# A transformer layer with a mixture of experts: three units' rows sorted by expert and computed in 15 groups of 256

## The chip, the cores and the metric

The kernel runs on one core of a Trainium2 chip. The metric is the device time of one execution in microseconds. Its engines are TensorE (PE in the rows, its weight loads PEld), VectorE (DVE), ScalarE (ACT), GpSimd (POOL) and the queue of SyncE (SP), each with its own instruction queue that it works through in order. Engines wait for each other through semaphores.

## What is computed

16 sequences of 128 tokens (2048 rows of 192 numbers) pass an embedding, an attention layer with 8 wide heads, a second attention ("mixer") with 12 heads of 16, a dense feed-forward layer and a mixture of experts. The change touches the last one alone:

```python
xm = _ln(x, ln2_g, ln2_b)
logits = xm @ gate_w.T + gate_b                  # 4 experts
topv, topi = jax.lax.top_k(logits, TOPK)         # TOPK = 2
gates = jax.nn.softmax(topv, axis=-1)
comb = ...                                       # gates spread over the 4 experts, 0 for the two not chosen
for e in range(NEXP):                            # NEXP = 4
    he = jax.nn.gelu(xm @ exp_w1[e] + exp_b1[e], approximate=False)   # 192 -> 768
    oe = he @ exp_w2[e] + exp_b2[e]                                    # 768 -> 192
    moe_out = moe_out + comb[..., e:e + 1] * oe
return x + moe_out
```

Every row needs only two of the four experts; the reference computes all four and multiplies two of them by zero.

## The kernel before

**Tiles and units.** The 2048 rows are 16 tiles of 128 rows, 4 units of 4 tiles (`UNIT = 4`, so 512 rows). Attention comes first; `mixer_and_feed_forward` does the rest, in one block. Its work is cut in named steps, and the order of the steps on each engine is written out by hand for the first part (`ORDERS`, one list each for pe, act, dve and pool) and made by a rule for the rest (`order`, with the additional steps of `after` hung behind chunks).

**Precision.** A factor in 32 bits is split in a high part of a narrower type (`fp32r`) and the rest (`_hi`, `_lo`). Layer 1 of an expert (L1) is five matmuls of 512 rows for each chunk of 128 hidden values; there are 6 chunks (`HC = 6`). ScalarE then takes the gelu from PSUM (L1426) and makes the high part (L1430), VectorE subtracts to get the low part (L1570). Layer 2 (L2) is, for each of 4 tiles, one matmul against 384 columns (L1335, both parts of w2) and one against 192 (L1336), summed over the 6 chunks in the four banks of `ps_out`. Behind the sixth chunk VectorE adds the result, weighed by `gates`, to `total` in 8 operations (step EF, L1635 to L1639).

**Experts.** `ffns` lists 4 units x 4 experts, `chunks` has 96 entries: all units meet all experts. L2 runs two chunks behind L1 (`LAG = 2`). `hid_hi` and `hid_lo` have 3 buffers, `gelu` has 2, and all that TensorE writes besides `ps_scores`/`ps_out` goes through a ring of 4 PSUM banks (`slot_free` waits until the bank is emptied).

**Routing a unit.** EN normalises its rows (VectorE: bias, moments, 13 small steps of a root, then 4 scalings that write `xn`), EX transposes them (PE), scales and splits them (ACT L1412, L1414, DVE L1566), EG makes the logits, EB turns them back and subtracts the largest, RANK finds the two largest, EXP is the exponential (ACT, with a table load before it and one behind), GATES makes the weights. For units 1 to 3 these steps are spread over the last expert of the unit before and the first of its own. WEIGH sums the experts' output biases by the gates, on GpSimd (L1142, L1144). B adds the rows saved earlier (`h1`, loaded by SP) to the residual (L1132); the single buffer `h1` is loaded for the next unit only behind B of this one (`base_ready`).

**Weights.** SP loads the weights of the dense layer and the experts one after the other in `stage` and `stage2`; H (GpSimd, L1116 to L1120) and W (DVE, L1488) split them. `load_weights(f)` waits until the f-th earlier set is split (`weights_lo`). At the end `store` and four DMAs write `total` to `out`.

## Time and profile before

| | us |
|---|---|
| median of 3 runs | 876.88 (876.34 to 877.64) |
| the profiled execution | 875.9 |
| its span, first to last instruction | 874.1 |
| TensorE busy | 792.7 (91%) |
| VectorE busy | 534.2 (61%) |
| ScalarE busy | 475.8 (54%) |
| GpSimd busy | 275.1 (31%) |

The profile shows one execution. Busy times say which engine is short of time over the whole; a change in one stage has to be read from the time in which it lies. The stages on the clock of the trace: attention to about 423 us, mixer and dense layer from there to about 657, mixed with the first experts of unit 0 from 619, and experts alone to 871. A matmul row shows a start and a length; matmuls overlap, so the distance between starts is what one costs.

### The profile page before, as it was taken

The page shows a single profiled execution, that of the slowest core. Times are in us where ns is not written, and L with a number is a line of the kernel's source. Part 1 is how long each engine was busy: PE and PEld are TensorE (multiplying, and loading weights), DVE is VectorE, ACT ScalarE, POOL GpSimd, SP SyncE. Part 2 cuts the span into 40 slices and gives each one's busy share as a digit, 9 for nine tenths or more (in the row PEclk, how much of TensorE's full clock was granted, in tenths as well). Part 3 has the DMA queues.
Part 4 walks back from the last instruction along what each step waited for, and adds up shares of the span by engine and source line. Part 5 has one row for each costly group of instructions (what it writes and reads, how often), then busy time and mean ns, then how long its engine had stood idle before and what let it go on. Part 6 is the DMA issues. An engine that isn't in the chain of part 4 may idle for free.

```text
span 874.1 us, 16507 instructions
## 1 busy us (share of the span) xinstructions
PE 792.7 (91%) x6000; PEld 716.2 (82%) x6000; DVE 534.2 (61%) x1404; ACT 475.8 (54%) x1292; POOL 275.1 (31%) x483
## 2 busy tenths in 40 slices
PE   0398999999999999998388799999989999999998
PEld 0298999999999999997367688888888898888987
DVE  4855545546454545426587688765677766775565
ACT  2155444444544454543078488997635575666654
POOL 6363020201111110202133745555376053070060
PEclk9989999999999999999699699999999999999999
DMA  8253333241413142333402002000040000100000
GB/s 254 90 118 73 73 82 74 72 84 55 93 55 86 34 109 47 73 82 73 137 1 64 2 1 65 1 20 2 15 124 8 1 19 3 35 0 1 18 2 18
DMA packets 37505, 47.32 MB, mean 54 GB/s; under 512 B 4721, under 2 KB 32497, under 8 KB 37425
## 3 DMA queue, kind: packets, MB, share of 16 engines
q1 hardware_dynamic: 34608, 42.03, 19.1%
q0 software_dynamic: 944, 2.16, 1.0%
q10 hardware_dynamic: 1872, 2.08, 0.9%
q8 instruction: 48, 0.79, 0.4%
q14 instruction: 33, 0.26, 0.1%
HBM read 30.53 MB, written 15.73 MB: 53 GB/s over the span
## 4 chain that ended last, share of the span: by engine, by line
PE 37%; DVE 5%; POOL 4%; DMA 2%; ACT 2%; issue 1%; SPq 0%; ACTq 0%; DVEq 0%; POOLq 0%
PE mix_ring L1320 11%; PE mix_scores L1335 7%; PE mix_scores L1336 3%; PE mix_ring L1262 2%; PE mix_ring L1211 2%; PE mix_ring L1233 2%; PE mix_ring L1274 2%; PE mix_scores L1200 1%; PE mix_ring L1173 1%; POOL mix_bias_part L1142 1%; DMA mix_stage<-in_w 1%; PE mix_ring L1224 1%; ACT mix_probs L1377 1%; POOL mix_bias_sum L1144 1%; DMA mix_w_out<-in_w_mix_out 1%
## 5 line engine op out<-in xcount | busy, mean ns | idle before, releaser
L454 POOL TENSOR_SCALAR attn_probs<-attn_probs,attn_inverse 128x128 f32<-128x128 f32 x128 | 47.8, 374 | 288.3 <-DVE attn_inverse L744 280.5
L1570 DVE TENSOR_TENSOR mix_hid_lo<-mix_gelu,mix_hid_hi 128x512 fp32r<-128x512 f32 x96 | 80.5, 840 | 68.2 <-ACT mix_hid_hi L1430 67.4
L1335 PE MATMUL mix_scores<-mix_w,mix_hid_hi 128*128 128x384 f32 x384 | 115.9, 359 | 0.4 <-DVE mix_hid_lo L1570 0.3
L1426 ACT ACTIVATE mix_gelu<-mix_ring,mix_b 128x512 f32<-128x512 f32 x96 | 65.7, 684 | 86.4 <-PE mix_ring L1320 79.6
L1336 PE MATMUL mix_scores<-mix_w,mix_hid_lo 128*128 128x192 f32 x384 | 96.5, 251 | 0.0
L1102 POOL TENSOR_SCALAR mix_probs<-mix_probs,mix_inverse 128x128 f32<-128x128 f32 x192 | 73.5, 403 | 65.9 <-DVE mix_inverse L1528 65.9
L613 ACT ACTIVATE attn_probs<-ps_scores,attn_neg_max 128x128 f32<-128x128 f32 x128 | 45.2, 366 | 77.8 <-DVE attn_neg_max L740 77.8
L1335 PEld LDWEIGHTS mix_scores<-mix_w,mix_hid_hi 128*128 128x128 f32 x384 | 72.2, 188 | 5.8 <-DVE mix_hid_lo L1570 1.6
L1336 PEld LDWEIGHTS mix_scores<-mix_w,mix_hid_lo 128*128 128x128 f32 x384 | 73.1, 190 | 3.3
L1377 ACT ACTIVATE mix_probs<-mix_scores,mix_neg_max 128x128 f32<-128x128 f32 x192 | 67.6, 389 | 1.9 <-DVE mix_neg_max L1520 1.8
L1142 POOL TENSOR_SCALAR mix_bias_part<-mix_b,mix_gates 128x192 f32<-128x192 f32 x64 | 38.4, 614 | 94.7 <-DVE mix_gates L1606 93.6
L1430 ACT ACTIVATE mix_hid_hi<-mix_gelu 128x512 fp32r<-128x512 f32 x96 | 60.8, 633 | 9.8 <-PE mix_scores L1336 6.9
L627 ACT ACTIVATE attn_mixed_rows<-ps_mixed 128x512 f32<-128x512 f32 x32 | 19.3, 604 | 84.6 <-PE ps_pairs L544 84.6
L751 DVE COPY attn_mixed_rows<-ps_pairs 128x256 f32<-128x256 f32 x32 | 13.6, 424 | 66.4 <-PE ps_pairs L544 66.4
L559 PE MATMUL ps_scores<-w_proj_main,attn_mixed_rows 128*128 128x192 f32 x256 | 44.4, 326 | 2.5 <-issue 1.8
L559 PEld LDWEIGHTS ps_scores<-w_proj_main,attn_mixed_rows 128*128 128x128 f32 x256 | 41.8, 190 | 3.4 <-issue 2.0
L1377 ACT ACTIVATION_READ_ACCUMULATOR mix_probs<-mix_scores,mix_neg_max 128x1 f32 x192 | 44.2, 230 | 0.0
L1320 PE MATMUL mix_ring<-mix_xt_hi,mix_w_hi 128*128 128x512 f32 x96 | 40.7, 424 | 0.8 <-DVE hin L1556 0.8
L736 DVE TENSOR_TENSOR attn_v_flat<-ring,attn_b_v 128x512 f32<-128x512 f32 x48 | 32.8, 684 | 8.5 <-PE ring L503 8.3
L1320 PE MATMUL mix_ring<-mix_xt_lo,mix_w_hi 128*128 128x512 f32 x96 | 37.9, 394 | 0.0
L1320 PE MATMUL mix_ring<-mix_xt_lo,mix_w_stack 128*128 128x512 f32 x96 | 37.8, 394 | 0.0
L1320 PE MATMUL mix_ring<-mix_xt_hi,mix_w_stack 128*128 128x512 f32 x96 | 37.7, 392 | 0.0
(292 smaller groups left out, 2373.7 us busy)
## 6 DMA issues: line engine op xcount, KB each, us to landing
v_rows<-attn_v_flat SPq DMA_DIRECT2D x16, 768.0 KB, 3.3
attn_v_rows<-v_rows SPq DMA_DIRECT2D x128, 96.0 KB, 3.7
mix_stage<-in_w SPq DMA_DIRECT2D x5, 576.0 KB, 5.8
mix_stage<-in_w SPq DMA_DIRECT2D x10, 192.0 KB, 3.2
mix_stage<-in_w SPq DMA_DIRECT2D x5, 384.0 KB, 4.3
attn_stage_main<-in_w_qkv SPq DMA_DIRECT2D x2, 768.0 KB, 6.8
h_rows<-hin SPq DMA_DIRECT2D x8, 192.0 KB, 2.0
mix_h<-h_rows SPq DMA_DIRECT2D x4, 384.0 KB, 4.9
```

The costliest lines, as they stand in the source:

```text
L454: last = nc.gpsimd.tensor_scalar(probs[:, n, j, :], probs[:, n, j, :], inverse[:, n, j:j + 1], float(D) ** -0.5, ALU.mult, ALU.mult)
L559: last = nc.tensor.matmul(out_of(b), mixed_rows[:, c, :], w, start=c == 0, stop=c == KTILES - 1)
L613: last = nc.scalar.activation(probs[:, n, j, :], ps_scores[:, n % 2, j, :], ACT.Exp, bias=neg_max[:, n, j:j + 1], accum_out=sums[:, n, j:j ...
L1102: last = nc.gpsimd.tensor_scalar(turn, turn, inverse[:, i, s:s + 1], 1.0, ALU.mult, ALU.mult)
L1142: last = nc.gpsimd.tensor_scalar(bias_part[:, b, :], b2[:, 1 + e, :], gates[:, b, e:e + 1], 1.0, ALU.mult, ALU.mult)
L1320: last = nc.tensor.matmul(ring[:, bank("L1", i), :], w[:, cols], x[u % XSETS][:, part, :], start=n == 0, stop=n == 4)
L1335: nc.tensor.matmul(ps_out[:, b, 0:2 * D], hid_hi[:, i % 3, tile], w2[:, c, :, :], start=c == 0, stop=False)
L1336: last = nc.tensor.matmul(ps_out[:, b, 0:D], hid_lo[:, i % 3, tile], w2[:, c, 0, :], start=False, stop=c == HC - 1)
L1377: last = nc.scalar.activation(probs[:, h // 2 % 2, i, s, :], ps_scores[:, i, s * P:(s + 1) * P], ACT.Exp, bias=neg_max[:, i, s:s + 1], acc ...
L1426: nc.scalar.activation(gelu[:, i % 2, :], ring[:, bank("L1", i), :], ACT.Gelu, bias=b1[:, f * HC + c:f * HC + c + 1]).then_inc(chunk_read, 1)
L1430: nc.scalar.activation(hid_hi[:, i % 3, :], gelu[:, i % 2, :], ACT.Copy).then_inc(hi_ready, 1)
L1570: nc.vector.tensor_tensor(hid_lo[:, i % 3, :], gelu[:, i % 2, :], raw(hid_hi[:, i % 3, :]), ALU.subtract).then_inc(lo_ready, 1)
```

## The change

Unit 0 is computed as before, all rows with all four experts. Units 1 to 3 (1536 rows, 3072 pairs of row and expert) are sorted by expert in DRAM and computed in groups.

- **Routing in one place.** EX, EG, EB, RANK, EXP and GATES of units 1, 2 and 3 all hang behind the six chunks of unit 0's third expert (chunks 12 to 17). EN of unit 2 moves to the first steps. New steps: CNT (PE: 8 matmuls that count, for each row, the earlier rows that chose each expert), SLOT (8 small DVE operations that make the two slots of each row), TABLE (16 small DVE operations: expert and block of each group), SCATTER (GpSimd: 8 indirect DMAs for each unit, 128 rows of 197 numbers each: the normalised row, its 4 gates and its own number).
- **Prefill.** SP writes 28 blocks of 256 empty rows to `sorted` and one to `home`, between `load_h1(0)` and `load_weights(1)`; `pattern`, their source, lies in `xt_full`, so EX of unit 0 waits for it. `home` gets the residual rows (`set_home`).
- **Groups.** 15 groups of 256 rows. SP reads the group's block and expert from `table` into registers and loads its rows and biases (`load_group`, rows in 5 buffers). GW1 copies the expert's layer 1 weights to a fixed place: ScalarE the high part (768 columns), VectorE the two others (1536 columns). GX transposes the rows (6 matmuls), ScalarE scales and splits, VectorE subtracts. G1 is a block: two chunks of 128 hidden values x 256 rows, ten matmuls of 256 rows; G2 its layer 2, eight matmuls, with w2 addressed by a register. GF (DVE, 6 operations) makes the weighed sum with the bias, GA (GpSimd) adds it to `home` with two indirect DMAs that add; GA of a group waits until the adds of the group before have landed.
- **End.** Unit 0's fourth expert (chunks 18 to 23) is computed behind the last group; SP then copies `home` to `out` and stores unit 0. The biases of unit 0 (WEIGH) are summed in groups 2 to 5.

```diff
-        for u in range(1, UNITS):
-            i = (u - 1) * NEXP * HC + (NEXP - 1) * HC
...
+        EARLY = 3 * HC
+        put(FIRST, ("EX", (1, 0)), ("EX", (1, 1)), ("EN", (2, NORM_PARTS - 1)))
+        put(FIRST + 1, ("EG", 1), ("EN", (3, 0)), ("EN", (3, 1)))
+        put(FIRST + 2, ("EB", 1), ("RANK", 1), ("EX", (2, 0)), ("EX", (2, 1)), *(("EN", (3, part)) for part in range(2, NORM_PARTS - 1)))
+        put(FIRST + 3, ("EXP", 1), ("CNT", 1), ("SLOT", 1), ("GATES", 1), ("SCATTER", 1), ("EG", 2), ("EN", (3, NORM_PARTS - 1)), ("B", 2), ("B", 3))
+        put(FIRST + 4, ("EB", 2), ("RANK", 2), ("EX", (3, 0)), ("EX", (3, 1)))
+        put(FIRST + 5, ("EXP", 2), ("CNT", 2), ("SLOT", 2), ("GATES", 2), ("SCATTER", 2), ("EG", 3))
+        put(FIRST + 5, ("EB", 3), ("RANK", 3), ("EXP", 3), ("CNT", 3), ("SLOT", 3), ("TABLE", 0), ("GATES", 3), ("SCATTER", 3))
...
+        both = [("L1", i) for i in range(FIRST - LAG, EARLY)] + [("G1", i) for i in range(len(blocks))] + [("L1", i) for i in range(EARLY, len(chunks))]
...
+            if step == "G1":
+                g, k = blocks[i]
+                if g + 1 < SORTS and k < 2:
+                    order.append((("GW1", "GX")[k], g + 1))
...
+            def load_group(g):
+                q = sp.value_load(table[0:1, 0, g:g + 1], min_val=0, max_val=NEXP * BLOCKS_OF - 1)
...
+            for q in range(NEXP * BLOCKS_OF):
+                sp.dma_start(dram["sorted"][q * GT:(q + 1) * GT, :].rearrange("(b p) r -> p b r", p=P), pattern).then_inc(prefilled, 16)
...
+            sp.wait_ge(scattered, 16 * TWO * UNIT * SORTED)
+            sp.wait_ge(table_ready, 1)
+            for g in range(SORTS):
+                load_group(g)
+            sp.wait_ge(came_home, 16 * GROUP_TILES * SORTS)
+            sp.dma_start(dram["out"][UT:TOKENS, :], dram["home"][0:SORTED * UT, :]).then_inc(out_stored, 16)
...
+            def scatter(u):
+                pool.wait_ge(xn_ready, u + 1)
...
+                for b in range(UNIT):
+                    for k in range(TWO):
+                        nc.gpsimd.indirect_dma_start(dram["sorted"], bass.IndirectOffsetOnAxis(ap=slots_at[:, u - 1, k, b:b + 1], axis=0),
+                                                     rows_of(u)[:, b, 0:ROW], None).then_inc(scattered, 16)
...
+            def bring_home(g):
+                pool.wait_ge(group_free, GROUP_TILES * (g + 1))
...
+                    pool.wait_ge(came_home, 16 * GROUP_TILES * g)
+                for b in range(GROUP_TILES):
+                    nc.gpsimd.indirect_dma_start(dram["home"], bass.IndirectOffsetOnAxis(ap=group_rows[:, g % DEEP, b, ROW - 1:ROW].bitcast(I32), axis=0),
+                                                 group_y[:, g % 2 * GROUP_TILES + b, :], None, compute_op=ALU.add).then_inc(came_home, 16)
...
+            def group2(i):
...
+                if k == 0:
+                    expert[g] = pe.value_load(table[0:1, 1, g:g + 1], min_val=0, max_val=NEXP - 1)
...
+                        nc.tensor.matmul(to[:, 0:2 * D], hid_hi[:, mine, tile], w_all[:, bass.ds(expert[g], 1), W1 + col:W1 + col + 2 * D], start=k + c == 0, stop=False)
...
+            def put_weights(g):
...
+                nc.vector.tensor_copy(w_dense[:, g % 2, HID:W1], raw(w_all[:, bass.ds(e, 1), HID:W1].rearrange("p e n -> p (e n)"))).then_inc(weights_put, 1)
```

## Rows read from the trace of the kernel before

**Rows 1.** Windows: length, busy (count) of PE, PEld, DVE, ACT, POOL, clock, DMA share, GB/s.
```profile
478.00:486.00 8.00, 0.51 (x5) 0.30 (x3) 2.69 (x6) 1.20 (x3) 4.52 (x8) 0.74 0.35 119
486.00:495.00 9.00, 8.98 (x56) 7.70 (x57) 5.07 (x8) 4.82 (x16) 7.09 (x11) 0.50 0.00 0
...
661.00:871.00 210.00, 208.56 (x1198) 183.97 (x1197) 138.49 (x310) 125.17 (x189) 63.90 (x71) 1.00 0.03 8
```

**Rows 2.** Timeline, PE: start, length. First L1 and L2 matmul of a chunk, next chunk.
```profile
848.95 0.42 PE L1320 MATMUL mix_ring<-mix_xt_hi,mix_w_hi 128*128 128x512 f32 x1
...
850.13 0.34 PE L1335 MATMUL mix_scores<-mix_w,mix_hid_hi 128*128 128x384 f32 x1
...
851.26 0.42 PE L1320 MATMUL mix_ring<-mix_xt_hi,mix_w_hi 128*128 128x512 f32 x1
```

**Rows 3.** Timeline, PE: two neighbours of the dense layer's matmuls of 256 rows.
```profile
617.21 0.28 PE L1262 MATMUL mix_ring<-mix_dxt_hi,mix_w_hi 128*128 128x256 f32 x1
617.33 0.28 PE L1262 MATMUL mix_ring<-mix_dxt_lo,mix_w_hi 128*128 128x256 f32 x1
```

**Rows 4.** Timeline, PE: two tiles of rows turned between these two starts.
```profile
630.26 0.27 PE L1237 MATMUL mix_ring<-ident,hin 128*128 128x128 f32 x1
...
631.46 0.44 PE L1335 MATMUL mix_scores<-mix_w,mix_hid_hi 128*128 128x384 f32 x1
```

**Rows 5.** Timeline, PE: where unit 0's chunk 12 begins.
```profile
661.19 0.42 PE L1320 MATMUL mix_ring<-mix_xt_hi,mix_w_hi 128*128 128x512 f32 x1
```

**Rows 6.** Timeline, DVE: start of an EF of eight operations, and what follows it.
```profile
664.74 0.73 DVE L1636 SCALAR_TENSOR_TENSOR mix_total<-mix_scores,mix_gates,mix_total 128x192 f32<-128x192 f32 x2
...
667.40 0.69 DVE L1570 TENSOR_TENSOR mix_hid_lo<-mix_gelu,mix_hid_hi 128x512 fp32r<-128x512 f32 x1
```

**Rows 7.** Timeline, DVE: small operations, each waiting for the one before, three steps apart.
```profile
700.40 0.22 DVE L1593 TENSOR_TENSOR mix_ties<-mix_ties,mix_earlier 128x64 f32<-128x64 f32 x1
...
701.17 0.17 DVE L1596 TENSOR_SCALAR mix_chosen<-mix_rank 128x16 f32<-128x16 f32 x1
```

**Rows 8.** Timeline, POOL: indirect DMAs of the embedding, one behind the other.
```profile
4.46 0.97 POOL L414 DMA_INDIRECT hin<-in_token_emb,attn_ids  x1 [0.30 <-issue]
5.74 0.94 POOL L414 DMA_INDIRECT hin<-in_token_emb,attn_ids  x1 [0.30 <-issue]
```

**Rows 9.** DMA view: issues, KB of each, median us from issue to landing.
```profile
v_rows<-attn_v_flat SPq DMA_DIRECT2D x16, 768.0 KB, 3.3
...
mix_h<-h_rows SPq DMA_DIRECT2D x4, 384.0 KB, 4.9
...
hin<-in_token_emb,attn_ids POOLq DMA_INDIRECT x16, 4.9
...
mix_b_qk<-in_b_mix_qk ACTq DMA_DIRECT2D x1, 1.5 KB, 1.7
```

**Rows 10.** Lines view, busy and mean ns: GpSimd's B, ACT's gelu and high part.
```profile
L1132 POOL TENSOR_TENSOR hin<-hin,mix_h 128x768 f32<-128x768 f32 x4 | 7.4, 1840 | 25.8 <-DVE norm_zn L1666 25.8
...
L1401 ACT ACTIVATE mix_dgelu<-mix_ring,mix_b 128x256 f32<-128x256 f32 x48 | 19.6, 472 | 9.3 <-PE mix_ring L1262 9.1
...
L1430 ACT ACTIVATE mix_hid_hi<-mix_gelu 128x512 fp32r<-128x512 f32 x96 | 60.8, 633 | 9.8 <-PE mix_scores L1336 6.9
```

**Rows 11.** Source view: shortest, median and longest ns of a DVE copy of 256 columns.
```profile
L187 DVE COPY norm_zn<-norm_zn x4: 293/294/349, 420.3 to 512.4; 128x256 f32<-128x256 f32 x4
```

**Rows 12.** Source view: the same of the low part on DVE.
```profile
L1570 DVE TENSOR_TENSOR mix_hid_lo<-mix_gelu,mix_hid_hi x96: 674/692/2228, 622.9 to 867.9; 128x512 fp32r<-128x512 f32 x96
```

**Rows 13.** Timelines of POOL, SP, DVE: start, length; [idle before and what ended it].
```profile
433.62 1.16 POOL L1116 TENSOR_SCALAR mix_w_hi<-mix_stage 128x768 fp32r<-128x768 f32 x1 [8.20 <-DMA mix_stage<-in_w]
...
474.53 1.78 SPq L1049 DMA_DIRECT2D mix_stage<-in_w  x2
...
639.69 0.96 DVE L1488 TENSOR_TENSOR mix_w_lo<-mix_stage,mix_w_hi 128x768 fp32r<-128x768 f32 x1 [4.30 <-POOL mix_w_hi L1116]
```

**Rows 14.** Source view: L2's second matmul, with its first and last start.
```profile
L1336 PE MATMUL mix_scores<-mix_w,mix_hid_lo x384: 247/252/255, 627.0 to 869.8; 128*128 128x192 f32 x192
```

More of the change, by code:

```diff
@@ L962, in mixer_and_feed_forward, with second_of @@
         order = []
-        for i in range(FIRST, len(chunks)):
-            chunk(i)
-        for i in range(len(chunks) - LAG, len(chunks)):
-            second(i)
+        blocks = [(g, k) for g in range(SORTS) for k in range(BLOCKS)]
+        place = lambda i: i if i < EARLY else len(blocks) + i
+        both = [("L1", i) for i in range(FIRST - LAG, EARLY)] + [("G1", i) for i in range(len(blocks))] + [("L1", i) for i in range(EARLY, len(chunks))]
+        def second_of(step, i):
+            if step == "L1":
+                second(i)
+                return
+            g, k = blocks[i]
+            order.append(("G2", i))
+            if k == BLOCKS - 1:
+                order.append(("GF", g))
+                order.append(("GA", g))
+                if 2 <= g < 2 + NEXP:
+                    order.append(("WEIGH", (0, g - 2)))
+        for n, (step, i) in enumerate(both):
+            if n < LAG:
+                continue
+            if (step, i) == ("G1", 0):
+                second_of(*both[n - LAG])
+                second_of(*both[n - LAG + 1])
+                order.append(("GW1", 0))
+                order.append(("GX", 0))
+            order.append((step, i))
+            if step == "G1":
+                g, k = blocks[i]
+                if g + 1 < SORTS and k < 2:
+                    order.append((("GW1", "GX")[k], g + 1))
+            if not (step == "G1" and i < LAG):
+                second_of(*both[n - LAG])
+            if step == "L1":
+                order.extend(after.get(i, ()))
+        for step, i in both[-LAG:]:
+            second_of(step, i)
         slot_of, slots = {}, 0
         for step, i in first_steps["pe"] + order:
-            for part in range({"X": 1, "Q": 1, "V": 1, "T": HALF, "A": 1, "O": 1, "DX": 1, "D1": 1, "D2": 1, "EX": 1, "EG": 1, "EB": 1, "L1": 1}.get(step, 0)):
+            for part in range({"X": 1, "Q": 1, "V": 1, "T": HALF, "A": 1, "O": 1, "DX": 1, "D1": 1, "D2": 1, "EX": 1, "EG": 1, "EB": 1, "L1": 1, "CNT": 1, "GX": 1, "G1": 1}.get(step, 0)):
                 slot_of[step, i, part] = slots
@@ new lines, in group1 @@
+            def group1(i):
+                g, k = blocks[i]
+                n = EARLY + i
+                act.wait_ge(l1_filled, n + 1)
+                act.wait_ge(lo_ready, n - 1)
+                if k == 0:
+                    act.wait_ge(group_weights[g % 3], 32 * (g // 3 + 1))
+                for c in range(2):
+                    part = slice(c * GT, (c + 1) * GT)
+                    last = nc.scalar.activation(gelu[:, n % 2, part], ring[:, bank("G1", i), part], ACT.Gelu, bias=group_b1[:, g % 3, 2 * k + c:2 * k + c + 1])
+                last.then_inc(chunk_read, 1)
+                act.wait_ge(chunk_read, n + 1)
+                act.wait_ge(hid_used, n - 2)
+                nc.scalar.activation(hid_hi[:, n % 3, :], gelu[:, n % 2, :], ACT.Copy).then_inc(hi_ready, 1)
```

436 lines of the change are left out of this document (318 added, 118 removed), and 4 rows, old and new, of the table ORDERS.

## The prediction

> **What bounds the kernel now.** I read the windows by stage first, then TensorE's timeline inside the stage that changes. From 661 us, where chunk 12 begins [rows 5], to 871 TensorE is busy 208.6 of 210.0 us at the full clock (2.4 GHz), with VectorE at 138.5, ScalarE at 125.2 and GpSimd at 63.9 [rows 1]. So the experts cost what TensorE needs for them: every chunk taken away is worth its TensorE time, and every wait of TensorE that is put in its place costs its whole length. One chunk is 1.18 us of L1 (848.95 to 850.13) and 1.13 of L2, together 2.31 [rows 2]. All before 661 stays nearly as it is.
>
> **What is saved on TensorE.** Chunks 24 to 95 go, 72 x 2.31 = 166.3 us. In their place come 15 groups x 3 blocks = 45 blocks. A block has ten matmuls of 256 rows at a pitch of 0.12 us [rows 3], 1.20 in all, and the same eight L2 matmuls as a chunk, 1.13 to 1.16: 2.36, so 45 x 2.36 = 106.2. Turning a group's two tiles costs 1.20 us (630.26 to 631.46) [rows 4]: 15 x 1.20 = 18.0. CNT, 8 small matmuls three times, is about 3. Net saving 166.3 - 106.2 - 18.0 - 3 = 39 us, not the 38% of the expert work that fewer rows suggest, since the groups are padded (3840 rows for 3072) and turned again.
>
> **What the sorting costs between chunk 17 and the first group.** No group can start before all 24 scatters have landed, and TensorE has no other work in its queue: L2 of chunks 16 and 17 is the last. So I follow the chain through the queues, from 661.2 on.
> Prices on VectorE: a low part 0.62 back to back (0.69 alone) [rows 12]; a small operation that waits for the one before, 0.26 for 64 columns and 0.20 for 4 to 16 (701.17 - 700.40 = 0.77 for three) [rows 7]; EF 2.65 (664.74 to 667.40) [rows 6]. In order: low part 12, EX(1), EN(2) to 668.8; low part 13, EF, EG(1), the first two parts of EN(3), a weight split to 676; low part 14, EB, RANK(1), EX(2), the root of EN(3), a weight split to 683; low part 15, SLOT(1) 1.3, GATES(1) 0.8 to 686.1. TensorE alone would be at that place before 680: VectorE has become the bound, since three units' routing lies in six chunks. It goes on through EN(3), EX(3), RANK(2), SLOT(2), EB(3), RANK(3), SLOT(3), TABLE (16 operations, 3.3 us) to GATES(3) at 705.6. TensorE ends L2 of chunk 17 at about 702.5.
> GpSimd is later still. An indirect DMA occupies it every 1.28 us (4.46 to 5.74) [rows 8]; I take 1.26, the mean of three distances there. SCATTER(1) runs 686.1 to 696.2. Then B(2), 1.84 [rows 10], to 698.1. B(3) is queued right behind it, and its `h1` is loaded by SP only after B(2): issue to landing 4.9 [rows 9], so 703.1; SCATTER(2) and SCATTER(3) are queued behind that wait. B(3) to 704.9, SCATTER(2) to 715.0, SCATTER(3) to 725.1. The last one issues at 723.9 and lands 4.9 later [rows 9]: 728.8. GATES(3), at 705.6, is then long done.
> SP reads a register and loads the group's rows, between the 3.3 and the 4.9 us of larger loads [rows 9], 4.4 with the register: 733.2. TensorE turns them, 1.2; ScalarE scales and splits, 2 x 0.47 + 0.63 = 1.6 [rows 10]; VectorE 0.69: the first block starts at about **737**, after 31 us without TensorE work.
>
> **The clock.** After the stretch 478 to 486 with TensorE almost idle, the granted clock stands at 0.50 (1.2 GHz) for 9 us in which it is busy [rows 1]. An idle stretch of 31 us should do the same: 9 us at half speed, 4.5 us lost. If the clock did not fall it would be 0; I keep both ends.
>
> **The group loop.** TensorE: 106.2 + 14 x 1.2 + chunks 18 and 19 of L1, 2.3 = 125.3. New and in no row: one register read of TensorE for each group, and w2 addressed by a register. For the read the rows give nothing (the queue has it ahead) to 1.7 us (the smallest load from memory) [rows 9]; I take 0.4, two small steps of 0.2 [rows 7], since it reads a few bytes of SBUF: 6 us for 15, with 0 to 25 as ends. The addresses I take at 0, hidden behind 0.29 us for each pair of matmuls, with 16 us (0.09 for each of 180 pairs) as the upper end. A group so costs TensorE 8.3 + 0.4 = 8.7 us.
> The cover for the rest is thin. VectorE in a group: three low parts 2.1; the weight copy of 1536 columns, by the 0.29 us of 256 columns [rows 11] about 0.95, or 1.75 at the rate of a low part; the group's input and gates 1.1; GF 2.3; its register 0.4; waits 0.3: 7.1 to 8.0. ScalarE: 3 x (0.94 + 0.63) + 1.6 + 0.9 for 768 columns + 0.4 = 7.6 [rows 10]. Both are under 8.7, so I add nothing. GpSimd: GA's two DMAs 2.5 and its wait for landing, 1.26 + 4.9 = 6.2 in all, also under 8.7.
>
> The low parts show that VectorE and GpSimd stand in each other's way: median 692 ns, longest 2228 [rows 12]. The Trainium skill (SBUF — State Buffer, on the shared port pair) says that an fp32 `tensor_copy` from SBUF to SBUF locks GpSimd out, which then cannot write DMA descriptors. This speaks against the weight copies; by it each GA could be late by one copy, which its slack of 2.5 us covers, and the sum stays. The Trainium skill (DMA: Bandwidth & Descriptors, latency and other measured facts) gives a `tensor_load` a floor of about 600 ns; by that page 15 reads would be 9 us instead of 6, if they are such loads, which no row shows.
>
> **The end.** The last G2 ends at 737 + 4.5 + 125.3 + 6 = 872.8. Then L1 of chunk 20, L2 of 18 behind GF (a stall of 0.6), and the rest: 12.2 us, TensorE ends at 885.0. Before, it ended at 870.05 [rows 14] and the span at 874.1, so 4.1 more: 889.1. Beside it the way home: GF 1.7, GA's issue 1.3, landing 4.9, copy of 1.18 MB about 6 (3.3 for 0.77 MB [rows 9]), 14 us behind the last G2 against 16.3: hidden. The profiled execution's own time is 875.9 for a span of 874.1, 1.8 more: **890.9 us**, against 875.9 there, which lies 0.1% under the median.
>
> **Edits at nothing.** GpSimd's additional fills lie in the 8.2 us in which it waits for the first weights, until 433.6 [rows 13]. The prefill (5.8 MB) stands behind those loads in SP's queue, and the second weights behind it, issued at 474.5 before [rows 13]: 41 us, of which it needs 25 at the 0.77 MB in 3.3 us of [rows 9], and 41 at 140 GB/s. Without that cover GpSimd's splits and probabilities would wait and TensorE with them, microsecond for microsecond. EN(2), 5 us of VectorE, goes mostly into the 4.3 us in which it waits until 639.7 [rows 13]; at worst 3 us. WEIGH moves under the groups.
>
> **The rivals.**
> 1. *The loop is bound beside TensorE or by registers.* VectorE at 8.0 plus contention, or addresses that do not hide, at 9.6 to 10.4 us a group: 14 to 26 us more, 905 to 917. For: thin cover, in-order waits (GF stands ahead of a low part). Against: double and triple buffers. 0.18.
> 2. *The adding DMAs bound the loop.* GA waits for the group before. It decides from 8.7 us, that is from a landing of 7.4; one of the embedding's took 7.7. An add has to read `home` first. At a landing of 10 the period is 11.3: 14 x 2.6 = 36 more, 927. 0.10.
> 3. *Faster: scattering is cheap.* If GpSimd issues a scatter every 0.5 us, SCATTER(3) ends with GATES(3), at about 710, the first block starts at 722, and with registers at nothing the sum is 891 - 15 - 6 = 870. It decides below 0.7 us each. Against: all 16 rows of this kind take 0.94 or more. It also covers the case that the saving is larger than I see. 0.17.
> 4. *The low ends together* (cadence 0.95, registers 0, clock 0): 891 - 7 - 6 - 4.5 = 874, and up to 882. 0.10, half of it within 0.2%.
>
> **How the numbers follow.** My own case, 882 to 900, has 0.45. The range reaches from half of rival 3 to past rival 1: 864 to 922. A measurement of this kernel can tell about 0.2% from no change (875.1 to 878.6). Faster 0.17, within 0.2% 0.05, slower 0.78.
>
> **What would show it.** Right: TensorE idle about 30 us behind unit 0's third expert, GpSimd with 24 indirect DMAs of 1.26 us and a wait for `mix_h` between them, clock 0.5 after it, G1's first start near 737, the same step 8.7 us later in each group. Wrong: a first group before 725, or groups apart by other than 8.3 to 9.2 us; waits of VectorE or GpSimd for the adds would name rival 2, low parts that end last rival 1.

## The result and the profile after

The median is 890.52 us (889.86 to 895.3, 4 runs) against 876.61 for the kernel before beside it: a ratio of 1.0171, 95% interval 1.0133 to 1.021. (The two medians alone give 1.0159; the ratio, taken over all runs, is above it because one of the four took 895.3.) The profiled execution takes 889.86 with a span of 888.1. The sum said 890.9 and 889.1. Two of its terms were off by more than the total shows, and in opposite directions.

The page's busy times, and windows of the new kernel (length, busy and count of PE, PEld, DVE, ACT, POOL, clock, DMA share, GB/s):

```profile
PE 768.2 (87%) x6072; PEld 696.4 (78%) x6072; DVE 539.8 (61%) x1468; ACT 481.8 (54%) x1341; POOL 304.2 (34%) x514
...
661.00:700.00 39.00, 33.49 (x210) 26.08 (x209) 30.80 (x107) 21.09 (x32) 10.14 (x7) 0.88 0.05 16
700.00:740.00 40.00, 10.30 (x43) 8.89 (x44) 10.98 (x42) 3.56 (x5) 21.04 (x21) 0.54 0.31 94
740.00:780.00 40.00, 40.00 (x291) 36.23 (x291) 24.62 (x49) 32.26 (x63) 11.60 (x8) 0.93 0.26 46
780.00:820.00 40.00, 40.00 (x310) 36.88 (x310) 31.87 (x64) 32.44 (x63) 32.52 (x29) 1.00 0.41 62
820.00:870.00 50.00, 49.45 (x367) 45.96 (x366) 34.48 (x77) 37.92 (x73) 23.45 (x13) 1.00 0.35 49
```

Where [rows 1] had one stretch of full TensorE work, there are now a hole (10.3 of 40 us busy from 700 to 740) and behind it a loop in which TensorE is busy all the time. TensorE does 24.5 us less work than before in the whole (768.2 for 792.7), though part of it at half clock, and the hole costs more than that.

The chain of work that ended last, through the hole (start, length, what):

```profile
688.02 3.16 POOL sorted_rows L1240
693.49 1.44 POOL sorted_rows L1240
701.28 1.83 POOL hin L1215
703.12 3.60 DMA mix_h<-h_rows
706.91 1.74 issue
714.18 1.62 POOL sorted_rows L1240
728.98 2.50 DMA sorted_rows<-mix_later_rows,mix_slots_at
732.47 2.53 DMA mix_group_rows<-sorted_rows
739.70 4.63 PE mix_ring L1487 x20
```

It is GpSimd's: scatters, B(2), the load for B(3), scatters, the last landing, the group's load. TensorE's timeline at the hole, three groups on (L1343 is the first matmul that turns a group's tile), and at the end:

```profile
735.05 0.48 PE L1343 MATMUL mix_ring<-ident,mix_group_rows 128*128 128x128 f32 x1 [26.74 <-DMA mix_group_rows<-sorted_rows]
739.70 0.58 PE L1487 MATMUL mix_ring<-mix_xt_hi,mix_w_dense 128*128 128x256 f32 x1 [2.51 <-DVE mix_xt_lo L1875]
...
752.12 0.27 PE L1343 MATMUL mix_ring<-ident,mix_group_rows 128*128 128x128 f32 x1
760.42 0.27 PE L1343 MATMUL mix_ring<-ident,mix_group_rows 128*128 128x128 f32 x1
768.72 0.27 PE L1343 MATMUL mix_ring<-ident,mix_group_rows 128*128 128x128 f32 x1
...
871.50 0.41 PE L1444 MATMUL mix_scores<-mix_w_all,mix_hid_hi 128*128 128x384 f32 x1 [2.05 <-issue]
```

From 752 on a group takes 8.30 us, each time the same. That is what 3 x 2.36 + 1.2 = 8.28 of [rows 2 to 4] gives for TensorE's matmuls alone: the register and the addresses it makes cost nothing there. VectorE's register work shows as a row of its own, beside the weight copy (shortest, median, longest ns):

```profile
L1970 DVEq FUSED_REGOPS  x15: 69/69/69, 713.9 to 851.8; - x15
L1970 DVE CAST mix_w_dense<-mix_w_all x15: 947/960/1193, 714.0 to 851.9; 128x1536 fp32r x15
```

The new DMAs (KB of each, median us to landing), where [rows 9] had only neighbours:

```profile
sorted_rows<-mix_xt_full SPq DMA_DIRECT2D x28, 197.0 KB, 8.0
mix_group_rows<-sorted_rows SPq DMA_DIRECT2D x15, 197.0 KB, 2.7
```

The scatters land in 2.5 us (median; the 4.9 of the embedding's gathers was my price) and the adds in 3.9.

### The profile page after: what moved, and what is told of

Read it like the earlier page. It is cut to its first block, busy times and chain, and to the rows that moved or that the text cites. A ratio compares the mean times of both kernels' runs of the same rounds, so it can differ in the third digit from the quotient of the medians.

```text
span 888.1 us, 17364 instructions
## 1 busy us (share of the span) xinstructions
PE 768.2 (87%) x6072; PEld 696.4 (78%) x6072; DVE 539.8 (61%) x1468; ACT 481.8 (54%) x1341; POOL 304.2 (34%) x514
## 4 chain that ended last, share of the span: by engine, by line
PE 35%; DVE 6%; POOL 4%; issue 2%; DMA 2%; ACT 2%; SPq 0%; ACTq 0%; DVEq 0%; POOLq 0%
PE mix_ring L1487 6%; PE mix_scores L1507 4%; POOL sorted_rows L1240 3%; PE mix_ring L1368 3%; PE mix_ring L1426 2%; PE mix_ring L1317 2%; PE mix_ring L1380 2%; PE mix_ring L1345 2%; PE mix_scores L1508 2%; PE mix_ring L1339 2%; PE mix_ring L1279 2%; PE mix_scores L1306 2%; PE mix_scores L1444 1%; PE mix_ring L1343 1%; PE mix_ring L1330 1%
## 5 line engine op out<-in xcount | busy, mean ns | idle before, releaser
L1251 POOL DMA_INDIRECT home_rows<-mix_later_rows,mix_group_rows x30 | 55.6, 1855 | 74.1 <-DVE mix_later_rows L1903 63.9
L1487 PE MATMUL mix_ring<-mix_xt_hi,mix_w_dense 128*128 128x256 f32 x270 | 58.4, 292 | 2.5 <-DVE mix_xt_lo L1875 2.5
L1507 PE MATMUL mix_scores<-mix_w_all,mix_hid_hi 128*128 x180 | 55.3, 363 | 0.0
L751 DVE COPY attn_mixed_rows<-ps_pairs 128x256 f32<-128x256 f32 x32 | 13.6, 425 | 65.9 <-PE ps_pairs L544 65.9
L1638 ACT ACTIVATE mix_gelu<-mix_ring,mix_group_b 128x256 f32<-128x256 f32 x90 | 37.7, 470 | 22.7 <-PE mix_ring L1487 22.6
L1487 PE MATMUL mix_ring<-mix_xt_lo,mix_w_dense 128*128 128x256 f32 x180 | 49.9, 287 | 0.0
L1487 PEld LDWEIGHTS mix_ring<-mix_xt_hi,mix_w_dense 128*128 128x128 f32 x270 | 46.1, 194 | 3.3 <-DVE mix_xt_lo L1875 3.1
L1508 PE MATMUL mix_scores<-mix_w_all,mix_hid_lo 128*128 x180 | 45.1, 250 | 0.0
L1883 DVE TENSOR_TENSOR mix_hid_lo<-mix_gelu,mix_hid_hi 128x512 fp32r<-128x512 f32 x45 | 32.2, 718 | 20.8 <-ACT mix_hid_hi L1642 20.8
L539 PE MATMUL ps_mixed<-attn_pt,attn_v_rows 128*128 128x128 f32 x256 | 33.9, 275 | 2.5 <-DMA attn_v_rows<-v_rows 1.6
L1558 ACT ACTIVATE mix_pt<-mix_ring 128x384 f32<-128x384 f32 x64 | 28.6, 507 | 13.5 <-PE mix_ring L1317 13.2
L1507 PEld LDWEIGHTS mix_scores<-mix_w_all,mix_hid_hi 128*128 128x128 f32 x180 | 33.8, 188 | 2.3 <-issue 2.2
```

Source lines behind the costliest of these rows:

```text
L539: nc.tensor.matmul(ps_mixed[:, j, :], v_rows[:, b, g, 0:MAIN], pt[:, n % 2, j, :], start=True, stop=True)
L1251: nc.gpsimd.indirect_dma_start(dram["home"], bass.IndirectOffsetOnAxis(ap=group_rows[:, g % DEEP, b, ROW - 1:ROW].bitcast(I32), axis=0), g ...
L1487: last = nc.tensor.matmul(ring[:, bank("G1", i), to], w[:, cols], x[:, part, :], start=n + c == 0, stop=n == 4 and c == 1)
L1507: nc.tensor.matmul(to[:, 0:2 * D], hid_hi[:, mine, tile], w_all[:, bass.ds(expert[g], 1), W1 + col:W1 + col + 2 * D], start=k + c == 0, st ...
L1508: last = nc.tensor.matmul(to[:, 0:D], hid_lo[:, mine, tile], w_all[:, bass.ds(expert[g], 1), W1 + col:W1 + col + D], start=False, stop=k = ...
L1638: last = nc.scalar.activation(gelu[:, n % 2, part], ring[:, bank("G1", i), part], ACT.Gelu, bias=group_b1[:, g % 3, 2 * k + c:2 * k + c + 1])
```

## How the runs are compared

Up to GpSimd's split of the third set of expert weights (its last piece, 1.85 us, at 617.23 in the changed kernel) no instruction differs between the kernels below, yet the profiles reach it at times from 617.2 to 621.7: at 617.2 where the granted clock from 486 to 495 is 0.80 to 0.82, at 621.7 (e7_scatter_early) where it is 0.50 there, and in between where it is in between. So beside the ratio of whole runs I count from that row to the first group's load on SP and to the end of the span:

| kernel | to the first load | to the end | against the changed kernel | ratio to before (95%) |
|---|---|---|---|---|
| changed | 115.2 | 270.9 | | 1.0171 (1.0133 to 1.0210) |
| e1_base_behind | 113.6 | 269.1 | -1.8 | 1.0177 (1.0153 to 1.0201) |
| e9_base_and_sp | 107.5 | 263.0 | -7.9 | 1.0086 (1.0061 to 1.0112) |
| e6_base_ahead | 109.8 | 263.8 | -7.1 | 1.0119 (1.0098 to 1.0140) |
| e2_one_slot | 103.7 | 257.7 | -13.2 | 1.0073 (1.0045 to 1.0101) |
| e4_norm2_spread | 110.3 | 264.1 | -6.8 | 1.0127 (1.0105 to 1.0149) |
| e5_warm | 116.7 | 269.8 | -1.1 | 1.0181 (1.0157 to 1.0206) |
| e10_warm_all | 115.7 | 269.3 | -1.6 | 1.0208 (1.0176 to 1.0241) |
| e3_expert_in_gap | 115.7 | 266.1 | -4.8 | 1.0139 (1.0119 to 1.0159) |
| e7_scatter_early | 106.2 | 260.2 | -10.7 | 1.0066 (1.0045 to 1.0086) |
| e8_all | 101.7 | 251.2 | -19.7 | 0.9962 (0.9948 to 0.9976) |
| e11_norm3_late | 109.5 | 259.6 | -11.3 | 1.0071 (1.0051 to 1.0091) |

Each row of the table is one execution, and its end holds one more piece of the clock that no edit made. At the start of unit 0's last second layers TensorE has waited 2.05 us in all nine kernels that compute them there. In the next 4 us its clock is 0.57 to 0.68 in the changed kernel, e1 and e9, and 1.00 in e2, e4, e5, e6, e7 and e10; from there to the end it is 16.6 us in the first three and 15.0 to 15.1 in the other six. So 1.5 us of the fourth column is the changed kernel's clock there, in every row but those of e1 and e9, which share it. The column to the first load is free of it. The ratios average over the runs of a kernel, but their intervals are 2 to 3 us wide on either side.

## Experiments on the start of the groups

My theory: GpSimd's own queue sets when the groups start. Its rival: VectorE's routing or the landings do, and GpSimd only waits for them.

**B behind the scatters.**

```diff
-        put(FIRST + 3, ..., ("SCATTER", 1), ("EG", 2), ("EN", (3, NORM_PARTS - 1)), ("B", 2), ("B", 3))
+        put(FIRST + 3, ..., ("SCATTER", 1), ("EG", 2), ("EN", (3, NORM_PARTS - 1)))
-        put(FIRST + 5, ..., ("GATES", 3), ("SCATTER", 3))
+        put(FIRST + 5, ..., ("GATES", 3), ("SCATTER", 3), ("B", 2), ("B", 3))
```

> Only the place of B(2) and B(3) in GpSimd's order is changed: both behind SCATTER(3) in place of ahead of SCATTER(2). Theory (the start of the first group is set by GpSimd's own queue): the two B take 1.82 and 1.85 us and the wait for mix_h between them 3.75, 7.4 us in all, so the last scatter is issued at about 722.5 (not below GATES(3), at 711 in the changed kernel), the first G1 starts at about 732 in place of 739.7, and the time falls from 890.5 to about 883, 1.008 of the kernel before. Rival (VectorE's chain or the landing of something else sets the start): the scatters only wait for GATES, first G1 stays at 738 to 740, time 889 to 891. Point of decision: first G1 before 735.

The ratio did not move, as the rival had it. But GpSimd did what the theory said: the last scatter is issued at 724.19 and not 728.98, although all of this profile lies 3.3 us later. SP's timeline shows where it went (start, length):

```profile
727.01 0.36 SPq L1104 DMA_DIRECT2D mix_h<-h_rows  x1
727.41 5.49 SPq L1108 DMA_DIRECT2D home_rows<-hin  x2
734.10 0.40 SPq L1114 DMA_DIRECT2D mix_group_rows<-sorted_rows  x1
```

The store of unit 3's residual into `home` waits for B(3), and the load of group 0 stands behind it in SP's queue. My expectation had followed B through GpSimd's queue and not through SP's. So the wait was handed on, and to separate the two accounts SP's order was changed too:

```diff
             set_home(1)
-            load_h1(3)
-            set_home(2)
-            set_home(3)
...
                 load_group(g)
+                if g == 2:
+                    load_h1(3)
+                    set_home(2)
+                    set_home(3)
```

> As e1_base_behind (B(2) and B(3) behind SCATTER(3) on GpSimd), and in SP's order the load of mix_h for unit 3 and the stores of home for units 2 and 3 stand behind the loads of groups 0 to 2 in place of ahead of group 0. Theory (e1_base_behind gained nothing because SP stood 7 us at the store of unit 3's home, which waits for B(3), with the first group's load behind it): the load now follows the last scatter, issued at 724.2 there, by 3.5 us and comes at about 727.5 in place of 734.1; time 883 to 884, ratio 1.009. Rival (another thing held the load, such as the landing of the scatters or the table): load at 731 or later, time 889 or more.

```profile
725.49 0.40 SPq L1114 DMA_DIRECT2D mix_group_rows<-sorted_rows  x1
...
733.70 6.89 SPq L1108 DMA_DIRECT2D home_rows<-hin  x2
```

The load comes 7.7 us earlier from the common row, the end 7.9, the ratio is 1.0086 where 1.009 was expected. The other way round, B(2) early, needs no change on SP:

```diff
-        put(FIRST + 3, ("EXP", 1), ..., ("EN", (3, NORM_PARTS - 1)), ("B", 2), ("B", 3))
+        put(FIRST + 3, ("B", 2), ("EXP", 1), ..., ("EN", (3, NORM_PARTS - 1)), ("B", 3))
```

> Only the place of B(2) and B(3) in GpSimd's order is changed, the other way round than in e1_base_behind: B(2) goes ahead of SCATTER(1), where GpSimd waits 27 us for unit 1's gates, and B(3) stays ahead of SCATTER(2). Then neither the wait for mix_h nor B(2) stands between the scatters, and SP, which in e1_base_behind had the store of home for unit 3 (5.5 us, behind B(3)) ahead of the first group's load, gets through that store early. Theory (GpSimd's queue sets the start of the groups, and e1_base_behind only moved the wait to SP's queue): 1.82 + 3.75 = 5.6 us, SCATTER(2) starts at 703.5 in place of 709.1, the first group's load at 727 in place of 732.5, time 885, ratio to the kernel before 1.011. Rival (something else, VectorE's GATES or the landings, sets the start, which is why e1_base_behind gained nothing): load at 731 or later, time 889 to 891.

GpSimd's timeline (start, length):

```profile
671.68 2.21 POOL L1215 TENSOR_TENSOR hin<-hin,mix_h 128x768 f32<-128x768 f32 x1 [12.12 <-DVE mix_later_rows L1961]
...
702.66 1.82 POOL L1215 TENSOR_TENSOR hin<-hin,mix_h 128x768 f32<-128x768 f32 x1
```

B(2) lies in GpSimd's idle time at 671.68 and the row that waited for `mix_h` waits no more: load 5.4 us earlier, where 5.6 was expected, ratio 1.0119. The mechanism holds in both forms.

**Half of the scatters.** The second expert's rows are left out of `sorted`.

```diff
-                    for k in range(TWO):
+                    for k in range(1):
                         nc.gpsimd.indirect_dma_start(dram["sorted"], ...)
```

> Of each token's two rows only the first is written into the sorted rows (12 scatters in place of 24); the second expert's rows are left out, so the groups compute with rows of zeros for them. Nothing else is taken away. Theory (GpSimd's issue of the scatters is the price of the gap): 12 x 1.27 = 15.2 us less on GpSimd, but the last four scatters can't start before GATES(3) at 711, so the chain is then GATES(3) 711 + 4 x 1.27 + landing 2.5 to 4 + load 2.7 to 4 + turning and splitting 4: first G1 at 726 to 728, 12 to 14 us sooner, time 877 to 879, about 1.002 of the kernel before. Rival (it is the latency behind the last scatter or VectorE's chain): first G1 at 735 or later, time 886 or more.

The load comes 11.6 us earlier and the end 13.2 (11.7 without the clock at the end); the ratio is 1.0073 where 1.002 was expected, 8.6 us less than the changed kernel's, and the profiled run is the fastest of its four. Beside the wait for `mix_h` (3.69 us) GpSimd now waits once between its scatters. The row names no engine, but the last step of GATES(3) ends on VectorE at 712.86:

```profile
713.63 0.98 POOL L1240 DMA_INDIRECT sorted_rows<-mix_later_rows,mix_slots_at  x1 [4.20 <-issue]
```

So GATES(3) is in the way, as expected, and the start gains a little under the 12 to 14 us expected. A scatter costs GpSimd 0.97 and 0.30 between two, 1.27, as [rows 8] had it.

**Normalising unit 2.** EN(2) was one of my edits at nothing, "at worst 3 us". In the changed kernel's trace VectorE's small steps of it come out long, and TensorE waits behind them. VectorE, GpSimd and TensorE (start, length):

```profile
636.97 0.86 DVE L124 TENSOR_SCALAR mix_half<-mix_work 128x4 f32<-128x4 f32 x1
638.44 1.07 DVE L128 TENSOR_TENSOR mix_work<-mix_rstd 128x4 f32<-128x4 f32 x1
640.12 1.75 DVE L130 SCALAR_TENSOR_TENSOR mix_rstd<-mix_work,mix_rstd 128x4 f32<-128x4 f32 x1
...
640.04 1.81 POOL L1215 TENSOR_TENSOR hin<-hin,mix_h 128x768 f32<-128x768 f32 x1
...
645.63 0.58 PE L1368 MATMUL mix_ring<-mix_dxt_hi,mix_w_dense 128*128 128x256 f32 x1 [5.11 <-DVE hin L1775]
```

The step at 640.12 takes 1.75 us for 4 columns (0.16 alone) and ends with GpSimd's B. The Trainium skill (SBUF — State Buffer, Who interferes with whom) says that a VectorE instruction with two SBUF inputs contends with a GpSimd instruction that reads SBUF; the trace agrees, with 1.75 us beside 0.16. (The step at 636.97 has one input and took 0.86 us for 0.17: that sentence does not cover it.) The experiment moves the steps between low parts:

```diff
-... L1:5 EN:1.6 EN:2.0 EN:2.1 EN:2.2 EN:2.3 EN:2.4 EN:2.5 W:3.0 ...
+... L1:5 EN:1.6 W:3.0 ... EF:0 EN:2.0 L1:8 EN:2.1 L1:9 DF:7.0 EN:2.2 L1:10 DF:7.1 EN:2.3 L1:11 EN:2.4 EN:2.5
```

> Only the place of tile 2's normalising steps EN(2,0) to EN(2,5) in VectorE's order is changed: they stand between the low parts of chunks 5 to 11 of the expert work in place of one stretch ahead of chunk 12. Theory (VectorE's small operations, stretched by GpSimd's weight splits at 634 to 643, make TensorE wait 5.1 us at chunk 12): that wait goes to under 1, chunk 12 starts at about 659 in place of 662.6, and if VectorE's chain from there on moves with it, the time falls by 3 to 5 us to 886 or 887, 1.012 of the kernel before. Rival (the steps cost VectorE the same wherever they stand, and GpSimd's queue sets the gap): chunk 12 starts 0 to 2 us sooner and the time is 889 to 891.

Ratio 1.0127, 3.9 us less than the changed kernel's ratio; the load 5.0 us earlier. TensorE's longest wait from 636 to 660 is 1.15 us and not 5.11, and chunk 12 starts at 658.38 (659 expected). So EN(2) had cost about 4 to 5 us, above my bound, and through VectorE's chain it had moved all that follows. How much of that is the lengthening (the 13 steps of the root took 6.7 us there, 2.4 where unit 3's stand at 681) and how much the place, this experiment does not separate: it changed both.

## Experiments on the clock

Behind the hole the granted clock is at half (1.2 GHz) until about 745. I had priced that at 4.5 us.

```diff
             def group_rows_turned(g):
+                if g == 0:
+                    slot_free("GX", g)
+                    for _ in range(112):
+                        nc.tensor.matmul(ring[:, bank("GX", g), :], weights[4][0][:, 0:P], xt_hi[0][:, 0, :], start=True, stop=True)
                 pe.wait_ge(group_loaded[g % DEEP], 16 * (g // DEEP + 1))
```

> 112 matmuls of 512 rows, whose result nobody reads, are added to TensorE's queue ahead of its wait for group 0, so that it is busy in the gap from 708 to 735. Theory (the gap costs, beyond its length, the half clock behind it): the granted clock is 1.0 when the groups begin, the nine or so microseconds of TensorE at half clock from 735 to 746 become 5 to 6, and the time falls by 3 us, to about 887.5. Rival 1 (the half clock behind the gap is hidden, since the first group waits for the other engines anyway): same time within 1 us. Rival 2 (the added matmuls last beyond the landing of the first group's rows): later by what they run over; 112 x 0.22 = 24.6 us at the full clock end at 733, at the half clock up to 750, 10 us later.

No gain. The added matmuls ended at 734.8, TensorE was then idle for 3.15 and 2.51 us, and the windows show the clock at 1.00 from 709 to 737, 0.84 from 737 to 741 and 0.50 from 741 to 745: it was lost again. So a second kernel covers those two stretches as well, 126 matmuls and 11 more ahead of the first block:

```diff
+                if (g, k) == (0, 0):
+                    slot_free("G1", i)
+                    for _ in range(11):
+                        nc.tensor.matmul(ring[:, bank("G1", i), :], weights[4][0][:, 0:P], xt_hi[0][:, 0, :], start=True, stop=True)
```

> As e5_warm, but with 126 matmuls ahead of the wait for group 0 and 11 more between the turning of group 0 and its first block, so that TensorE has nearly no idle stretch from 709 to the first block; e5_warm left 3.2 and 2.5 us idle, and its clock was at half again from 740 to 746. Theory (two idle stretches of some 3 us were enough to lose the clock again, and the half clock costs what the trace shows): granted clock 1.0 throughout 709 to 755, the first group's start unchanged, the first block and the turning behind it at 1.8 in place of 5.6 us, so 2 to 3 us less than the changed kernel: 888, ratio 1.014. Rival (the stretch at half clock costs nothing, since the other engines' chain of the first group is as long): same time as the changed kernel, 890 to 891, ratio 1.017.

PE windows of this kernel (length, busy, clock, DMA share, GB/s), the last of its added matmuls and the turning of group 0 behind them, and its wait ahead of group 1:

```profile
742.00:745.00 3.00, 3.00 (x18) 1.00 0.51 102
745.00:748.00 3.00, 3.00 (x27) 1.00 0.42 103
748.00:752.00 4.00, 2.66 (x21) 1.00 0.00 0
...
719.65 20.56 PE L1468 MATMUL mix_ring<-mix_xt_hi,mix_w_all 128*128 128x512 f32 x90
740.05 0.27 PE L1343 MATMUL mix_ring<-ident,mix_group_rows 128*128 128x128 f32 x1
...
751.45 0.38 PE L1495 MATMUL mix_ring<-mix_xt_hi,mix_w_dense 128*128 128x256 f32 x1 [1.34 <-DVE mix_xt_lo L1883]
```

The clock is full from 714 to 760, and the kernel is no faster. From the first group's load to the turning of group 3, the loop's first regular point, it takes 26.64 us (736.74 to 763.38) against 27.95 in the changed kernel (732.47 to 760.42) and 27.76 to 27.95 in all nine kernels whose groups begin at half clock: 1.1 to 1.3 us less. In the first two blocks TensorE gains 2.0 us (2.44 for 4.43) and in the two turnings some more. It loses 1.34 of what it gains waiting for ScalarE and VectorE, whose chain from a group's turned rows to its low part takes the same at either clock (737.24 to 739.64 and 741.37 to 743.78).

This is not the whole price of the half clock, though, for the added matmuls ran over, which was rival 2 of e5_warm: TensorE turns group 0 3.31 us behind its load's issue, where it begins 2.58 behind it in the changed kernel. These 0.7 us and the 1.3 together are 2.0 us, my estimate of what the full clock would give if nothing had to be added to keep it.

Counted from the common row to the end the two kernels are 1.1 and 1.6 us below the changed one, but 1.5 of that is the clock at the very end. No gain shows in the ratios either (1.0181 and 1.0208 for 1.0171), whose intervals could hide one of 2 us.

## Experiments on what may fill the hole

```diff
-        EARLY = 3 * HC
+        EARLY = 4 * HC
...
+            sp.wait_ge(total_biased, 1)
+            for b in range(UNIT):
+                sp.dma_start(dram["out"][b * P:(b + 1) * P, :], total[:, b, :]).then_inc(out_stored, 16)
             sp.wait_ge(came_home, 16 * GROUP_TILES * SORTS)
             sp.dma_start(dram["out"][UT:TOKENS, :], dram["home"][0:SORTED * UT, :]).then_inc(out_stored, 16)
```

> The fourth expert of unit 0 (six chunks, 14 us of TensorE) is computed ahead of the groups in place of behind them; unit 0's bias is added in a step of its own between groups, and its rows are stored ahead of the copy of home. The scatters stay as they are. Theory (the 27 us without TensorE's work between chunk 17 and the first group are free to hold it, and what is behind the last group is only the way home): the two L1 within the loop's last group go (2.3 us), the last second layer ends at about 866, behind it 9.3 us to the copy's issue and 6.8 to the end: span 882, time 884, ratio 1.009; with the half clock of 708 to 745 shortened, up to 1.5 us less. Rival (the gap can't hold it, since VectorE's and GpSimd's steps for units 2 and 3 stand among its low parts, so that the scatters start later by as much): first group 3 us or more later, time 887 to 892.

The hole held the expert (first load 0.5 us later from the common row), but the time fell by 2.8 us by the ratios, 4.8 by the traces, and not by 6.5. GpSimd's timeline at the end shows the rest:

```profile
867.74 1.76 POOL L1253 DMA_INDIRECT home_rows<-mix_later_rows,mix_group_rows  x1 [2.69 <-DVE mix_later_rows L1905]
869.80 1.57 POOL L1253 DMA_INDIRECT home_rows<-mix_later_rows,mix_group_rows  x1 [0.30 <-issue]
874.08 1.57 POOL L1253 DMA_INDIRECT home_rows<-mix_later_rows,mix_group_rows  x1 [2.71 <-DMA home_rows<-mix_later_rows,mix_group_rows]
```

The last group's adds now wait for the landing of the group before: without two L1 in the last group its sum is ready 3.3 us sooner (135.6 us behind the first load for 138.9) and GA only 0.4. The copy to `out` is issued 144.3 us behind the first load where the changed kernel needs 144.9. What was gained is that nothing is left to store behind that copy (6.1 us from its issue to the end for 10.8, or for 9.3 where the clock at the end does not fall): of the 4.8 us by the traces 3.3 are the edit's.

**Unit 3's normalising behind GATES(1).** On top of e6_base_ahead:

```diff
-        put(FIRST + 1, ("EG", 1), ("EN", (3, 0)), ("EN", (3, 1)))
-        put(FIRST + 2, ..., *(("EN", (3, part)) for part in range(2, NORM_PARTS - 1)))
+        put(FIRST + 1, ("EG", 1))
+        put(FIRST + 2, ...)
-        put(FIRST + 3, ..., ("SCATTER", 1), ("EG", 2), ("EN", (3, NORM_PARTS - 1)), ("B", 3))
+        put(FIRST + 3, ..., ("SCATTER", 1), ("EG", 2), *(("EN", (3, part)) for part in range(NORM_PARTS)), ("B", 3))
-        put(FIRST + 5, ..., ("SLOT", 3), ("TABLE", 0), ("GATES", 3), ("SCATTER", 3))
+        put(FIRST + 5, ..., ("SLOT", 3), ("GATES", 3), ("SCATTER", 3), ("TABLE", 0))
```

> As e6_base_ahead, and in VectorE's order all of EN(3) stands behind GATES(1) in place of in front of it, and TABLE behind GATES(3). Theory: 5.0 us of VectorE (2.6 at 674, 2.4 at 681) no longer stand ahead of GATES(1), so SCATTER(1) starts at 683 in place of 688, and with the 5.6 us of e6_base_ahead the first group's load is at 722 in place of 732.5, time 880, ratio 1.005. Rival (EN(3) is then late for B(3), or TensorE stalls on the steps behind it): SCATTER(2) waits for B(3), gain no larger than e6_base_ahead's, 885.

Ratio 1.0066 (expected 1.005), load 9.0 us earlier than in the changed kernel (10.5 expected). SCATTER(1) came as said (4.9 us sooner from the common row); then GpSimd waited 3.31 us for GATES(2): a part of the gain turned into a wait on VectorE.

**All together.**

> All that is under test together: e7_scatter_early, e4_norm2_spread and e3_expert_in_gap. Theory (the terms add, since they lie in different stretches): 10.5 + 4.5 + 6 = 21 us less than the changed kernel, 869 to 870, ratio 0.992, faster than the kernel before. Rival (they overlap, since TensorE, which fills the gap with 14 us, ends it later than the first group's load when that comes 15 us sooner, and VectorE has the low parts of the fourth expert to do beside routing): 874 to 880, ratio 1.000 to 1.005.

12 runs, median 872.23: a ratio of 0.9962 (0.9948 to 0.9976), 0.4% faster than the kernel before and 18.3 us less than the changed kernel by the ratios. It lies between the theory (0.992) and the rival (1.000 at best); the load came 13.6 us sooner where 15 was expected. The parts were worth 4.6 (e7_scatter_early beyond e6_base_ahead), 4.6 (e6), 3.9 (e4) and 2.8 (e3) by the ratios, 15.9 together. By the traces, less 1.5 us of clock in each, they are 9.2 (e7, with e6 in it), 5.3 (e4) and 3.3 (e3), 17.8 together, and e8_all is 18.2. So they add, as closely as either measure can tell. The windows say what is left (PE alone; the last is the way home):

```profile
690.00:730.00 40.00, 32.43 (x168) 0.83 0.26 78
...
855.00:871.00 16.00, 0.85 (x6) 0.57 0.44 98
```

**Unit 3's routing later.** The last kernel moves unit 3's turning and routing two chunks later than in e8_all:

```diff
-        put(FIRST + 4, ("EB", 2), ("RANK", 2), ("EX", (3, 0)), ("EX", (3, 1)))
+        put(FIRST + 4, ("EB", 2), ("RANK", 2))
-        put(FIRST + 5, ..., ("SCATTER", 2), ("EG", 3))
-        put(FIRST + 5, ("EB", 3), ("RANK", 3), ...)
+        put(FIRST + 5, ..., ("SCATTER", 2), ("EX", (3, 0)), ("EX", (3, 1)))
+        put(FIRST + 6, ("EG", 3))
+        put(FIRST + 7, ("EB", 3), ("RANK", 3), ...)
```

> As e8_all, with unit 3's turning, logits and routing two chunks later. In e8_all TensorE waited 5.6 us at 687.6 for unit 3's normalised rows, which stand behind GATES(1) there, and GpSimd waited 3.8 us for GATES(2) at 698.8. Theory (that one stall makes GATES(2) late, and GpSimd's scatters set the start of the groups): SCATTER(2) follows B(3) at 695 without a wait, the first group's load comes at 718.5 in place of 722.3, time 868.5, ratio 0.992. Rival (GATES(3), now two chunks later, becomes the last thing: above 709 it holds SCATTER(3)): load at 722 or later, time 872 or more.

The rival was right, 1.0071. GpSimd at SCATTER(2) and SCATTER(3); then the first matmul of CNT(3) and VectorE behind it:

```profile
694.33 1.34 POOL L1243 DMA_INDIRECT sorted_rows<-mix_later_rows,mix_slots_at  x1 [2.88 <-DVE mix_later_rows L1831]
...
713.67 0.98 POOL L1243 DMA_INDIRECT sorted_rows<-mix_later_rows,mix_slots_at  x1 [8.63 <-DVE mix_later_rows L1831]
...
707.28 0.61 PE L1460 MATMUL mix_ring<-mix_chosen,mix_before_any 128*128 128x16 f32 x2 [5.17 <-DVE mix_chosen L1821]
...
710.97 0.16 DVE L1841 TENSOR_TENSOR mix_run<-mix_ring,mix_run 128x4 f32<-128x4 f32 x1 [3.74 <-PE mix_ring L1464]
```

GATES(3) came 8.63 us after GpSimd was ready for it. With GpSimd's own waits gone, the chain of routing steps is the bound, and it is one order for three units: a step put behind is late for somebody. VectorE is not full in it (busy 10.3 of the 20 us from 694 to 714). Unit 3's logits first wait behind an EF of 2.6 us in VectorE's queue; then VectorE waits 3.74 us for CNT(3), which takes TensorE 3.4 us at half clock (0.50 from 707 to 711), where CNT(2) of the changed kernel takes 1.7 at the full one. Here a lost clock does stand in the chain.

## Why the prediction was right, step by step

- **Saving on TensorE.** A chunk pair and a block cost what [rows 2, 3] said: the loop's period is 8.30 us against 8.28. TensorE's busy time fell by 24.5 us and not by 39, in part because CNT took 8.1 us for 3 and several stretches ran at half clock.
- **VectorE becomes the bound, SCATTER(1) at 686.1.** It came at 688.02. TensorE waited 5.11 us ahead of chunk 12, where I had put nothing and allowed 3. Chunk 12 began only 1.4 us late (662.63 for 661.19 [rows 5]), because this execution came to the stage 2.7 us sooner: its clock was 0.80 from 486 to 495, where [rows 1] has 0.50. (ScalarE's operations of the two kernels lie 0.03 us apart at 491 and 2.7 at 500.) The step that failed is EN(2) at nothing; e4_norm2_spread shows its size.
- **GpSimd's chain.** Right in kind, shown by e6, e9 and e2. In size: the first scatter took 3.87 us for 0.96 (+2.9), each unit's row numbers 0.4, against that the wait for `mix_h` 3.75 for 4.9. GATES(3) came at 710.9 for 705.6, with GpSimd still 9 us from needing it. The last scatter is issued at 728.98, not 723.9; it lands in 2.5, not 4.9, and SP issues the load a microsecond later. Load landed and first block: 739.70 against 737, so 2.7 late. Errors of 2 to 5 us each way cancelled here.
- **The clock: right in TensorE's time, too large for the result.** Its cause is there (0.50 from 720 to 745). At half clock the turning of group 0 took 0.9 us longer up to ScalarE's start (2.19 for 1.32 in e10_warm_all), and the loop took 3.1 us more than the 125.3 of its matmuls: 4.0 for the 4.5 forecast. But e10_warm_all gives only 1.3 us back, 2.0 without its own overrun. A TensorE at half clock costs its whole excess only where TensorE is what all wait for, and in the first group it is so in part. What I had not seen is that the clock falls earlier too: it is 0.57 from 680 to 685 and 0.50 from 700 to 705, L1 of chunk 15 takes 2.1 us for 1.18, and TensorE ends L2 of chunk 17 at 708.3, not 702.5. No cost of that shows, since VectorE up to SCATTER(1) and GpSimd behind it were later still.
- **The loop: the term that was mis-sized.** I added 6 us for register reads. The rows had no such operation, I bounded it from both sides and took a value near the low end; zero would have been right. From the first block to the last G2 it took 128.4 us (739.7 to 868.1) and not 135.8, 6 of the 7.4 less from this. SP, which has nothing to hide them behind, shows a gap of 0.8 us between a load's end and the next issue (732.87 to 733.68), where it reads the expert. The Trainium skill (DMA: Bandwidth & Descriptors, Latency and other measured facts) gives a `tensor_load` some 600 ns; the gap on SP is near it, but no cost of it on TensorE shows.
- **The end.** I expected a stall of 0.6 at L2 of chunk 18. GF(14) stands in VectorE's queue between two low parts, so it ended at 871.4, and L2 began 3.4 us behind the last G2; then the clock fell again (0.61 from 871 to 875), which is 1.5 us that six of the later kernels did not pay. TensorE ended at 883.8, the span at 888.1, 20.0 behind the last G2 and not 16.3: 3.7 late.
- **The sum.** 2.7 - 7.4 + 3.7 = -1.0: 888.1 for 889.1. That the total is so near is luck: errors of 3 to 7 us cancelled, and the clock behind 486 and at the end was of one kind in this execution and of another in others.
- **Edits at nothing.** The prefill took 22.7 us of SP's queue (430.8 to 453.5) and the second weights were issued at 474.57, as before; GpSimd's fills were hidden in its wait, 6.2 us of which are left. The copies (0.96) and ScalarE's part took no time of TensorE's. An add of GpSimd with a copy beside it took 2.04 us (784.47, the copy from 785.47 to 786.43) and the next, without one, 1.58; whether the copy is the cause was not tried, and the period of the groups does not show it.
- **The rivals.** Loop bound elsewhere: VectorE is busy 31.9 of 40 us, no. Adding DMAs: landing 3.9, well under the 7.4 from which they decide, and GpSimd busy 1.86 us with each (1.26 assumed), though at the very end, in e3 and e8, it is their wait that counts. Cheap scatters: 1.27 each, no; e2 shows what they would have brought.
